# First cross-attention of a gated block: one load of 128 partitions a tile, in the order of use, and the last two tiles turned ahead of most theta products

## What is computed

```python
x = x + tanh(g_xattn[0]) * L0_xattn(ctx, ctx, layernorm(x))   # long convolution, 32 heads
x = x + tanh(g_ffn[0])   * L0_ffn(layernorm(x))               # int8 feed-forward
x = x + tanh(g_xattn[1]) * L1_xattn(layernorm(x), ctx)        # theta = theta_w @ ctx + theta_b
x = x + tanh(g_ffn[1])   * L1_ffn(layernorm(x))               # ternary weights
```

## Time and profile before

| | |
|---|---|
| median of 3 runs | 667.97 us (667.48 to 669.15) |
| the profiled execution | 668.62 us, span 666.8 us |
| granted TensorE clock, mean | 0.979 |
| TensorE busy | 614.3 us (92%) |
| VectorE, ScalarE, GpSimd busy | 546.9, 485.2, 346.7 us |

### The profile page before, as it was taken

The page is one execution under the profiler, slowest core; times in us unless marked ns, Lnnn a source line. Parts: engine busy times, 40 slices in busy tenths (PEclk is TensorE's granted clock), DMA queues, the critical chain, the costliest instruction groups (busy, mean ns, idle before and its releaser), DMA issues.

```text
span 666.8 us, 9517 instructions
## 1 busy us (share of the span) xinstructions
PE 614.3 (92%) x2811; PEld 362.0 (54%) x2842; DVE 546.9 (82%) x1069; ACT 485.2 (73%) x724; POOL 346.7 (52%) x436
## 2 busy tenths in 40 slices
PE   6489999999996969999999899999897999999997
PEld 6467787777774434545444555555442444444443
DVE  2428998899998669897778898889988899999865
ACT  2335779786865449899774456767679999999984
POOL 1418898887874245420000100013378898898951
PEclk9889999999998969999999999999999999999999
DMA  7996788999977934714918970000123676666561
GB/s 201 238 270 204 240 284 295 327 323 328 310 299 272 271 108 103 199 54 138 362 65 158 191 189 16 16 32 1 32 61 83 183 178 176 181 184 186 173 158 48
DMA packets 128822, 118.92 MB, mean 178 GB/s; under 512 B 84416, under 2 KB 91344, under 8 KB 127632
## 3 DMA queue, kind: packets, MB, share of 16 engines
q1 hardware_dynamic: 121024, 103.71, 54.8%
q10 hardware_dynamic: 7760, 14.76, 6.9%
HBM read 68.04 MB, written 30.49 MB: 148 GB/s over the span
## 4 chain that ended last, share of the span: by engine, by line
PE 62%; ACT 12%; DVE 11%; DMA 6%; issue 4%; SPq 4%; POOL 1%; DVEq 0%; ACTq 0%; POOLq 0%
PE ps L1240 18%; PE ps L1505 13%; PE ps L1521 8%; PE ps L1333 6%; ACT turn L1019 4%; PE ps L1432 3%; PE ps L1462 3%; DMA arena<-in_x 2%; ACT arena L969 2%; PE ps L1480 2%; PE ps L1251 2%; PE ps L1436 2%; SPq L379 2%; DMA arena<-in_ctx 1%; DVE amax L1732 1%
## 5 line engine op out<-in xcount | busy, mean ns | idle before, releaser
L1240 PE MATMUL ps<-arena 128*128 128x288 f32 x640 | 163.2, 411 | 6.2 <-ACT arena L794 1.7
L1240 PEld LDWEIGHTS ps<-arena 128*128 128x128 f32 x640 | 120.0, 192 | 39.0 <-issue 6.4
L1505 PE MATMUL ps<-arena 128*128 128x512 bf16 x510 | 113.4, 379 | 3.7 <-DVE arena L2098 3.4
L738 POOL TENSOR_TENSOR arena<-arena 128x512 f32<-128x512 f32 x64 | 80.4, 1276 | 9.1 <-DVE arena L2098 8.4
L1505 PEld LDWEIGHTS ps<-arena 128*128 128x128 bf16 x512 | 49.5, 98 | 65.6 <-issue 3.3
L633 POOL TENSOR_TENSOR arena<-arena 128x1024 f32<-128x1024 f32 x31 | 58.8, 1896 | 22.3 <-PE ps L1251 14.0
L1333 PE MATMUL ps<-arena 128*128 128x512 bf16 (+1 forms) x248 | 58.3, 390 | 2.2 <-DVE arena L1776 1.4
L1521 PE MATMUL ps<-arena 128*128 128x512 bf16 x241 | 57.1, 379 | 3.5 <-DMA arena<-hq_d 1.6
L1374 PE MATMUL ps<-arena 128*128 128x512 bf16 x250 | 55.3, 379 | 0.7 <-DVE arena L1847 0.4
L640 POOL TENSOR_TENSOR turn<-turn 128x512 f32<-128x512 f32 x31 | 39.7, 1282 | 24.0 <-DVE turn L1667 24.0
L2098 DVE SCALAR_TENSOR_TENSOR arena<-ps,up_scale,arena 128x512 f32<-128x512 f32 x64 | 46.8, 745 | 6.1 <-ACT arena L1109 5.3
(11 more groups left out here) (225 smaller groups left out, 1304.4 us busy)
## 6 DMA issues: line engine op xcount, KB each, us to landing
arena<-in_L_ffn_w SPq DMA_DIRECT2D x48, 512.0 KB, 5.5
arena<-kpad_d ACTq DMA_DIRECT2D x16, 512.0 KB, 5.0
hq_d<-arena SPq DMA_DIRECT2D x14, 512.0 KB, 3.0
tern_d<-late SPq DMA_DIRECT2D x24, 256.0 KB, 4.8
arena<-in_L_ffn_w ACTq DMA_DIRECT2D x8, 512.0 KB, 5.8
arena<-in_ctx SPq DMA_DIRECT2D x2, 2048.0 KB, 12.2
x_d<-arena SPq DMA_DIRECT2D x16, 256.0 KB, 3.9
arena<-x_d SPq DMA_DIRECT2D x4, 1024.0 KB, 7.6
```

The source lines that it names most:

```text
L738: pool.tensor_tensor(hg[:, s, sl], hh[:, s, sl], g3[:, sl], ALU.mult).then_inc(S["hg_done"], 1)
L1240: last = pe.matmul(ps[:, 4 * s + lo, 0:NB * PAIRS], toep[:, u, (LB - 1 - lo + li) * P:(LB - lo + li) * P], kv[:, s, li, :], start=(li == 0 ...
L1505: last = pe.matmul(ps[:, bank, :], xq4T[:, s, 4 * j + k, :], w[:, k, c * L:(c + 1) * L], start=(k == 0), stop=(k == LB - 1))
```

## The change

Eleven things change.

1. A load moves one whole tile: 128 partitions, 256 KB, from a source pattern of 4 blocks by 32 rows by 512 columns (`tile_rows`). Order: x 0, 1; context 2, 3; after `k_stored` context 4 to 7; x 2, 3; context 8 to 12; x 4 to 7; context 13, 14; x 8, 9; context 15; x 10 to 15. Context 0, 1 stay on ScalarE's queue.
2. There are more semaphores, and waits for fewer loads at a time. `x_stats0` waits at tiles 0, 2, 4 (for x 4 to 9) and 10. The groups of x tiles are 2, 2, 4, 4, 4.
3. `late` is ordered q2, q3, c13, c14, q4, q5, c15, q6 and on.
4. TensorE turns context tiles 4 and 5 before head 0, two more pairs within it. Tile 5 is copied by ScalarE. VectorE takes the statistics of x 0 and 1 before the first pairs. `norm_x0(1)` comes before `pairs(2, 0)`.
5. theta_w and b1 are loaded after b2 and turned after head 31, into a free bank, not in the opening.
6. `ctx_early[0]` moves to 32 to 48 KB, which holds the turned context of heads 0 to 15, and `xn1[1]` to 48 to 64 KB. It is loaded after the last w1 chunk, at head 23.
7. `w1_turned` is issued at w1 chunks 5, 6, 7; one remains for the end. ScalarE widens three quarters (heads 23, 25, 27), GpSimd one.
8. `x_normal` runs in heads 4 (two tiles) and 6 to 15.
9. The second group of `normalise_x1` moves from heads 28 and 29 behind the loop.
10. Two theta products stand ahead of the last two turns, not three.
11. The saves of x1 move one tile of 128 partitions each, to a target pattern of 4 by 32 by 512.

```diff
-        xn1 = [... for at in (112, 32)]
+        xn1 = [... for at in (112, 48)]
-        ctx_early = [... for at in (48, 160)]
+        ctx_early = [... for at in (32, 160)]
-        W1_WIDEN = (23, 27)
+        W1_WIDEN = (23, 25, 27)
-        on_dve = (1, 3, 5, 7)
+        on_dve = (1, 3, 7)
-        late = [None] + [("q", n) for n in range(2, 6)] + [("c", n) for n in range(13, NT)] + [("q", n) for n in range(6, NT)]
+        late = [None, ("q", 2), ("q", 3), ("c", 13), ("c", 14), ("q", 4), ("q", 5), ("c", 15)] + [("q", n) for n in range(6, NT)]
-        def both_halves(rows, gg, b):
-            return rows.rearrange("(s b) (g c) l -> b g c s l", b=G, c=CG)[b, gg]
+        def tile_rows(rows, n):
+            return rows.rearrange("(s b) (g c) l -> s g b c l", b=G, c=CG)[n % 2, n // 2]
+        def tile_home(m):
+            return m
+        def load_ctx(eng, tiles, done):
+            for n in tiles:
+                eng.dma_start(tile_home(ctx_raw[n]), tile_rows(ctx_d, n)).then_inc(done, 16)
...
+            def load_x(tiles, done):
+                for n in tiles:
+                    sp.dma_start(tile_home(x_res[:, order1[n], :]), tile_rows(x_d, n)).then_inc(done, 16)
...
+                    if k == WC - 1:
+                        sp.wait_ge(S["cd_ready"], HEADS // 2)
+                        sp.dma_start(ctx_early[0], ctx_rows[:, 0:NT // 2, :]).then_inc(c_in[0], 16)
...
-            sp.wait_ge(S["cd_ready"], HEADS)
-            sp.dma_start(ctx_early[0], ctx_rows[:, 0:NT // 2, :]).then_inc(c_in[0], 16)
...
+                for n in range(NT):
+                    if order1[n] in range(NT)[ffn_slots(i)]:
+                        at = n // 2 % G * CG
+                        first = n % 2 * 2 * G + n // 2 // G
+                        sp.dma_start(x1_d[at:at + CG, first:first + 2 * G - 1:2, :].rearrange("c b l -> b c l"),
+                                     tile_home(x_res[:, order1[n], :])).then_inc(S["x1_saved"], 16)
...
-                    done = {0: (0, 4), 2: (1, 8), 6: (2, 12)}[n]
+                    done = {0: (0, 2), 2: (1, 2), 4: (2, 6), 10: (3, 6)}[n]
...
-                if h < 10:
-                    x_stats0(6 + h)
+                if h < 12:
+                    x_stats0(4 + h)
```

More of the change, by code:

```diff
@@ L202, in flamingo_gated_block @@
         TC, WC = 3 * FF * L // (2 * P * L), FF * L // (2 * P * L)
-        ctx_early = [cut(at, NT // 2 * L).rearrange("p (t l) -> p t l", t=NT // 2) for at in (48, 160)]
+        ctx_early = [cut(at, NT // 2 * L).rearrange("p (t l) -> p t l", t=NT // 2) for at in (32, 160)]
         th_raw = cut(143, 2 * P).rearrange("p (d k) -> p d k", d=2)
@@ L257, in flamingo_gated_block @@
         x_in = [sem(f"x_in{g}") for g in range(NG)]
-        c_in = [sem(f"c_in{g}") for g in range(5)]
-        C_FIRST, X_FIRST = (4, 4), (4, 8, 12, 2)
+        c_in = [sem(f"c_in{g}") for g in range(6)]
+        C_FIRST, X_FIRST = (2, 2), (2, 2, 6, 6)
         xT_in = [sem(f"xT_in{s}") for s in range(2)]
@@ L646, in _ @@
             pairs(1, 1)
+            norm_x0(1)
             pairs(2, 0)
-            norm_x0(1)
             for h in range(HEADS - 3):
@@ L892, in _ @@
             repeat_q(0, 0)
+            open_copy(8)
+            toep_load(1, 1)
+            open_copy(9)
             repeat_c(2, 0)
-            for m in range(8, len(opening)):
+            for m in range(10, len(opening)):
                 open_copy(m)
-            act.wait_ge(S["th_tr"], 1)
-            act.activation(b1[:, :], ps[:, open_bank(len(opening)), 2 * P:2 * P + FT], ACT.Copy)
-            act.activation(th_w.rearrange("p d k -> p (d k)"), ps[:, open_bank(len(opening)), 0:2 * P], ACT.Copy).then_inc(S["th_made"], 1)
             x_normal(2)
@@ L915, in _ @@
                 if h == 4:
-                    act.wait_ge(S["small_in"], 64)
+                    act.wait_ge(S["small_in"], 96)
                     act.activation(tg[:, :], gates[:, :], ACT.Tanh).then_inc(S["tanh_done"], 1)
[L918 to L924, removed]
+                if h == 4:
+                    x_normal(4)
+                    x_normal(5)
+                if 6 <= h < NT:
+                    x_normal(h)
+                if h in (FIRST_TURN + G + 3, FIRST_TURN + G + 4):
+                    n = 2 * (h - FIRST_TURN - G - 3)
+                    normalise_x1(n)
+                    normalise_x1(n + 1)
                 for n in w1_at(W1_LOAD, h):
@@ L947, in _ @@
             act.activation(b2b[:, :], b2b[:, :], ACT.Copy, scale=tg[:, 2:3]).then_inc(S["b2_ready"], 1)
+            for n in X1_GROUPS[1]:
+                normalise_x1(n)
+            act.wait_ge(S["th_tr"], 1)
+            act.activation(b1[:, :], ps[:, 3, 2 * P:2 * P + FT], ACT.Copy)
+            act.activation(th_w.rearrange("p d k -> p (d k)"), ps[:, 3, 0:2 * P], ACT.Copy).then_inc(S["th_made"], 1)
+            for b in range(2):
+                theta_out(b)
             for n in X1_GROUPS[2]:
                 normalise_x1(n)
-            for b in range(4):
+            for b in range(2, 4):
                 theta_out(b)
@@ L1277, in _ @@
                 if h == 0:
[L1278 to L1284, removed]
+                    open_tiles(range(10, len(opening)))
             def theta(b):
@@ L1297, in theta @@
                 last.then_inc(S["th_tr"], 1)
-            for b in range(3):
+            pe.wait_ge(S["small_in"], 96)
+            pe.wait_ge(S["prod_done"], HEADS + 1)
+            pe.wait_ge(S["x1_dve"], TAIL - 1)
+            for d in range(2):
+                pe.transpose(ps[:, 3, d * P:(d + 1) * P], th_raw[:, d, :], identf[:, :])
+            pe.transpose(ps[:, 3, 2 * P:2 * P + FT], b1n, identf[0:FT, 0:FT]).then_inc(S["th_tr"], 1)
+            for b in range(2):
                 theta(b)
@@ L1307, in _ @@
                 last.then_inc(S["back_tr"], 1)
-            for b in range(3, NB):
+            for b in range(2, NB):
                 theta(b)
@@ L1615, in _ @@
             open_copy(1)
+            for n in X0_GROUPS[0]:
+                x_stats0(n)
             first_pairs()
             open_copy(3)
-            for n in X0_GROUPS[0]:
-                x_stats0(n)
-            open_copy(5)
             v.wait_ge(S["rs0"], 1)
```

95 lines of the change are left out of this document (34 added, 61 removed).

## The result

The changed kernel takes 737.98 us (median of four), the kernel before 668.56 us beside it: ratio 1.103, 95% interval 1.100 to 1.107. That is 69.4 us slower. The forecast was 50 us slower, with a range of 695 to 741 us, that is 27 to 73 slower. (Three executions lie at 737.37 to 738.14 us; the fourth, in a slower state at 868.82 us, is left out of the ratio.)

The account below looks back on a forecast made before the run. TensorE, busy 92% of the span, was taken as the bound except at the start and after head 31. 40.6 + 16.7 - 6.9 = +50.4 on 668.62 us gave 719.0, said as 718; the case's range 696 to 740.

Parts of the forecast that it names:

- Four engines, always the same: Tile loads and saves: outermost count 4 puts each on the same four engines, 97 GB/s, 2.71 us a tile.
- Term A: Opening: VectorE's head 1 waits for 25 tiles and three Toeplitz loads, starting at 76.1 instead of 47.25 us, +28.9.
- Term B: First ternary weights, behind all tiles, arrive at 99.0; head 5's products begin at 102.8, +40.6 us, with term A included.
- under the wait of term A: Opening's reordered edits, 1 to 3 us each, hidden by VectorE's wait for x before head 1; otherwise up to 3 together.
- Term C: Saves of x1: ScalarE waits for all 16, until 293.8, before gelu(2, 0) due at 277.06; +16.7 us.
- Term D: End of the heads: context load off the path, fewer theta products first; add of tile 14 at 216.0, not 222.90, -6.9.
- At nothing: Edits counted as free, among them context load and one more transpose in the ternary stream, two heads ahead; uncovered, 5 us.
- 5 or so: Allowance above the sum for roughly seen waits: SP's queue filling up, a slow clock after long idle stretches.
- the 711 that it gave for 2.56: Total forecast at 2.56 us a tile: B loses 4.8 and C 2.4, 711 us.
- slower engines (734): Total forecast at 3.03 us a tile: B gains 10.2 and C 5.1, 734 us.
- The rivals: All 16 engines, 648 us, chance 0.14; four engines but saves hidden, 702, 0.12; change does little, 665, 0.04.

Follow-up runs that it names:

- e1: Changed kernel with each tile load reading 128 successive DRAM rows (wrong rows, same bytes and order), saves as changed; 685.11 us.
- e5: Changed kernel with each x and context tile load split in two of 64 partitions, two blocks each; 816.45 us.
- e6: e3 with the old order of normalisations (old groups and heads of x_stats0, norm_x0, x_normal); wrong rows; 656.02 us.
- e3: Changed kernel with e1's loads of 128 successive rows (wrong rows) and the old saves of 32 partitions by 4 tiles; 665.51 us.
- e7: Kernel before with only items 6, 9 and 10, ctx_early[0] loaded behind the last ternary load; 659.55 us, ratio 0.9872.
- e8: Changed kernel with e4's loads, old saves, old normalisation order, context load behind the last ternary load, third transpose kept in the stream; 653.57 us, ratio 0.9767.
- e4: Changed kernel with loads of 32 partitions by two tiles in the new order with finer waits, and the old saves; 672.19 us, ratio 1.0058.
- e9: e8 with the third transpose of w1 behind the loop again and its widening on GpSimd; 652.48 us, ratio 0.9750.
- e2: Changed kernel with the old saves of x1, 32 partitions by 4 tiles; 721.08 us.

## Why the prediction was right, and where it fell short

- **Four engines, always the same.** Right, and shown by e1 and e5. 2.71 us a tile was forecast. Most issues in the chain take 2.46 us for a load and 2.45 for a save, but the nine from 41.34 to 64.50 take 23.16 together, 2.57 a tile, which fits the 101 to 104 GB/s. The Trainium skill, "DMA: Bandwidth & Descriptors", section "Why a DMA increments its semaphore by 16 and not by 1", gives this rule (the largest number up to 16 that divides both outermost counts, from the lowest engine up); the runs agree with the number at counts of 4 and 2, with shares of 0.26 and 0.13. The Trainium skill, "DMA: Bandwidth & Descriptors", section "Specifications", has about 27 GiB/s (29 GB/s) an engine; measured are 101/4 = 25.2 GB/s, 13% less.
- **Term A**, head 1 at 76.1 (+28.9): 75.80, +28.6. That it is so exact is in part luck. At 2.57 a tile the 25 tiles gained 3.5 us on the forecast; the share of 0.26 was reached only after 4 us where 2.5 was taken for the start, and the other 2 are not isolated.
- **Term B**, head 5's products at 102.8 (+40.6): they began at 109.26 (+46.9), and VectorE's head 5 came 48.5 late. This is the step that fell short, by 7.9 us. The first weights came 2.6 late (ScalarE starts on them at 101.64, 99.0 was forecast), which is near. The term took x_normal(4) to follow ScalarE's copies at once. It follows the scales of x 4 to 7, which GpSimd makes after head 6's pairs, and those wait for the copies: ScalarE idles 4.0, and from landing to products it is 3.7 more than forecast. The last 1.6 come behind the products' start. Head 5's twenty products took 6.67 us in the chain, where a head took 4.85 to 5.09 in the kernel before; after a stretch without products the granted clock was 0.50 in 100 to 109 us and 0.75 in 109 to 116.
- **What was not priced: the order of the normalisations.** The forecast put its edits in the opening (`norm_x0(1)` before `pairs(2)` and others) at nothing or up to 3 us together, "under the wait of term A", and gave the later heads of `x_stats0` and `x_normal` no price at all. By e6 against e3 the order costs 9.5 us net with fast loads. In the changed kernel they are the 4.0 of head 5 (already counted) and 8.9 at heads 10 to 14. There the scales of x 8 stand on GpSimd behind the pairs of head 10, and TensorE turns x 8 beside head 10; x 12 and head 14 stand so too. The timeline of the changed kernel before head 10:

```profile
135.58 1.02 POOL L603 TENSOR_TENSOR rstd<-ve,mhalf 128x4 f32<-128x4 f32 x1
...
136.91 0.81 ACT L789 ACTIVATE arena<-arena,shift,rstd 128x512 f32<-128x512 f32 x1 [4.50 <-POOL shift L605]
...
139.46 6.78 PE L1240 MATMUL ps<-arena 128*128 128x288 f32 x20 [1.94 <-issue]
```

  In the kernel before `x_normal(h + 1)` ran one head earlier from scales made heads before (`norm_x0` after heads 3 and 7 for x 6 to 9 and 10 to 13).
- **Term C**, the saves (+16.7): the wait was 15.3 in the trace, and undoing the saves gave 16.9, of which 16.5 stand behind head 31. Right. The 16 saves took 44.8 us from first issue to the gelu (301.47 to 346.27) where 46.4 was forecast.
- **Term D**, the end of the heads (-6.9): -6.7 from head 31's lag of 60.8 to the add's 54.1, and -6.6 by e7. Right, and its cover too: the two theta products and the turned theta weights show up nowhere in the chain.
- **At nothing, the stream of ternary loads ("uncovered, 5").** It was uncovered: 4.6 us at head 29. The third transpose holds SP for 8.12 us where 5.23 was taken, then comes the context load of 2 MB, and only then the load that ScalarE wants next. The timeline of the changed kernel there, and one line of its chain:

```profile
226.00 8.12 SPq L436 DMA_TRANSPOSE arena<-w_d  x1
...
235.42 0.47 SPq L425 DMA_DIRECT2D arena<-in_L_ffn_w  x1
...
245.48 1.15 ACT L875 ACTIVATE late<-arena,inv_s 128x1024 int16<-128x1024 f32 x1 [5.21 <-DMA arena<-in_L_ffn_w]
...
237.68 10.29 DMA tern_d<-late
```

  ScalarE wanted these weights from 240.27 on, 4.9 us after their issue: the stream did not run two heads (10.6 us) ahead here. The load took 10 us and the store beside it 10.29, with the DMA share at 1.04 to 1.07 in 235 to 252 us. With the context load behind the stream (e8), and the transpose kept, nothing is lost.
- **The sum.** Forecast +50.4. Add 7.9 in term B, 8.9 at heads 10 to 14, 4.6 at head 29, less 1.2 won by head 31, 1.4 less in C and 0.2 more in D: 69.4. The allowance of "5 or so" named SP's filling queue and a slow clock; of the three misses only a part of the first is of that kind. The others are an order on GpSimd that was given no price and a stream that was taken as covered. That 737.98 lies within the range is in part luck too. With the measured 2.57 a tile terms B and C are together 6.7 us smaller, so the forecast's own sum comes to the 711 that it gave for 2.56. The upper end was made of slower engines (734) and the 5, and neither is what filled it. The rivals fell: stores are dealt out like loads, the opening's share was 0.26 and not 1.05, and the change did not do little.

What stays open: how the 1.6 us of term B and parts of the losses at heads 3, 10 and 29 divide between clock and wait, and whether the context load would stall head 29 without the transpose; no run isolates them.

## What to carry to other kernels

Before a load is widened to 128 partitions, look at the outermost count of both its patterns: 4 blocks by 32 rows moved a quarter of what 128 rows did, and halving the blocks halved it again. A gain at the start reaches the end only if no later stage hands work over just in time. Here, of a head start of 9.9 us (e4), 8.8 were lost at head 5 to scales computed behind other work on GpSimd; with each tile normalised one head sooner the start was smaller, 5.8 us, but 5.3 of it lasted (e8). When a load is moved earlier, put it behind the stream that feeds the critical engine, not into it: behind a long transpose and ahead of the ternary loads the context load went with a stall of 3.4 to 6.0 us at head 29, and behind them with none.

## What the runs showed of the hardware that was not expected

- SP's issue of a load took nearly as long as the transfer of a tile in the changed kernel: 2.46 us each at 2.57 a tile. In e1, whose loads are of the same size, it took 0.47 (the last six of x in 2.81, at 18.20). So in the changed kernel SP's list ran at the pace of the transfers, and what stood behind the tiles was held too: the first ternary load was issued at 91.95, in e1 at 26.53.
- Loads of 32 partitions for two tiles moved 238 GB/s in e4 and 230 in e9 at a share of 1.07 to 1.08, while 128 successive rows moved 383 to 387 at 1.05. The kernel before moved 238 in the same window with another order of the loads. Between the two, the partitions of a load and the addresses of its rows both differ, so no run says which of them gives the higher rate.
- The first two transposes of w1 held SP for 4.45 to 5.83 us in every kernel. Where the third, with the same shape, follows in the same stream, it held SP for 7.85 (e2) to 8.88 (e1); why, no run tells.
- The granted clock in 10 to 20 us was 0.66 in e1 and 0.83 in e3, which have the same opening, and it moved VectorE's head 1 by some 3 us.
